# Post-LN stack with two attentions: transposing only the visible 64 by 64 of one probability block

## The reference, cut to what matters

```python
# x: 16 sequences x 256 tokens x 128; 16 heads of 64
h = silu(x @ W1.T + b1) @ W2.T + b2
q, k, v = split(h @ Wg.T + bg)
dots = einsum('bhid,bhjd->bhij', q, k) * 64 ** -0.5
mask = j >= i + 64                      # i: query, j: key
attn = softmax(where(mask, -inf, dots))
out = einsum('bhij,bhjd->bhid', attn, v) @ Wo.T + bo
```

## Time and profile before

| | |
|---|---|
| median of 3 runs | 1578.63 us (1572.71 to 1580.39) |
| the profiled execution's own time | 1580.31 us |
| span of its trace | 1578.5 us |
| busy: PE, PEld, DVE, ACT, POOL | 82%, 61%, 67%, 61%, 50% |
| first attention, about | 39 to 690 us |

### The profile page before, as it was taken

The page is one execution under the profiler, slowest core; times in us unless marked ns, Lnnn a source line. Parts: engine busy times, 40 slices in busy tenths (PEclk is TensorE's granted clock), DMA queues, the critical chain, the costliest instruction groups (busy, mean ns, idle before and its releaser), DMA issues.

```text
span 1578.5 us, 36791 instructions
## 1 busy us (share of the span) xinstructions
PE 1297.7 (82%) x9486; PEld 970.0 (61%) x9486; DVE 1055.8 (67%) x3800; ACT 959.6 (61%) x2716; POOL 796.1 (50%) x913
## 2 busy tenths in 40 slices
PE   7999999999999999836999999604778787787870
PEld 3766666666666666526999999602445455454540
DVE  1677777777777777738766666415777777777646
ACT  5877777777777777614555555302566656566654
POOL 1567777777777777749100000366665655552103
PEclk9999999999999999968999999855899989899985
DMA  9100000000000000021222222122423233232101
GB/s 346 48 8 14 13 13 12 13 12 13 13 13 13 12 12 14 14 81 44 60 66 67 67 67 66 55 52 50 84 50 76 55 69 60 48 76 37 31 1 53
DMA packets 77060, 75.02 MB, mean 48 GB/s; under 512 B 10913, under 2 KB 66977, under 8 KB 75330
## 3 DMA queue, kind: packets, MB, share of 16 engines
q1 hardware_dynamic: 67506, 56.86, 14.1%
q0 software_dynamic: 8192, 16.79, 3.8%
q10 hardware_dynamic: 1296, 0.59, 0.1%
HBM read 46.87 MB, written 27.33 MB: 47 GB/s over the span
## 4 chain that ended last, share of the span: by engine, by line
PE 30%; issue 6%; DVE 6%; ACT 6%; DVEq 3%; POOL 2%; POOLq 1%; SPq 1%; DMA 0%; ACTq 0%
PE psum L818 7%; PE psum L827 6%; PE psum L860 4%; PE psum L849 3%; PE psum L924 3%; ACT qst L1096 2%; POOL yk L568 2%; PE psum L940 2%; PE psum L941 1%; ACT wall L1052 1%; DVE wA L1303 1%; ACT wall L1096 1%; PE psum L882 1%; PE psum L804 1%; DVE xgT L1310 1%
## 5 line engine op out<-in xcount | busy, mean ns | idle before, releaser
L503 POOL TENSOR_SCALAR P<-P,rinv 128x192 f32<-128x192 f32 (+1 forms) x384 | 308.5, 816 | 167.1 <-DVE rinv L1168 165.4
L1008 ACT ACTIVATE P<-shifted,least 128x192 f32<-128x192 f32 (+1 forms) x512 | 240.2, 471 | 128.2 <-DVE least L1154 126.7
L1042 ACT ACTIVATE hid<-psum,wA 128x128 f32<-128x128 f32 x576 | 164.1, 368 | 129.2 <-PE psum L818 129.1
L1352 DVE TENSOR_REDUCE mx<-psum 128x2 f32<-128x512 f32 x256 | 164.5, 686 | 82.1 <-PE psum L924 78.4
L1154 DVE CUSTOM_DVE_ANT_0 shifted<-psum,band 128x192 f32<-128x192 f32 (+1 forms) x512 | 168.8, 385 | 30.6 <-PE psum L696 30.4
L1052 ACT ACTIVATE wall<-psum 128x1024 f32<-128x1024 f32 x128 | 131.0, 1024 | 84.6 <-PE psum L849 82.2
L818 PE MATMUL psum<-xgT,wA 128*128 128x128 f32 x1152 | 158.4, 281 | 13.0 <-DVE xgT L1310 12.3
L493 POOL DMA_INDIRECT xs<-x1c,pos x128 | 127.9, 999 | 56.1 <-issue 28.3
L827 PE MATMUL psum<-wB,hid 128*128 128x128 f32 x1152 | 153.3, 277 | 0.0
L818 PEld LDWEIGHTS psum<-xgT,wA 128*128 128x128 f32 x1152 | 141.6, 193 | 17.4 <-DVE xgT L1310 12.1
L568 POOL DMA_INDIRECT yk<-ys,posc x128 | 124.0, 969 | 49.0 <-issue 33.5
(11 more groups left out here) (246 smaller groups left out, 2678.4 us busy)
## 6 DMA issues: line engine op xcount, KB each, us to landing
xg<-xs SPq DMA_DIRECT2D x144, 64.0 KB, 1.8
ys<-yrow SPq DMA_DIRECT2D x72, 128.0 KB, 1.9
wall<-in_wall SPq DMA_DIRECT2D x1, 8232.0 KB, 36.7
qkd<-parts SPq DMA_DIRECT2D x32, 192.0 KB
qst<-qkd SPq DMA_DIRECT2D x66, 64.0 KB
wall<-qkd SPq DMA_DIRECT2D x35, 64.0 KB
kst<-qkd SPq DMA_DIRECT2D x11, 192.0 KB
hT<-in_xT SPq DMA_DIRECT2D x4, 512.0 KB, 5.6
```

What stands on the lines that cost most here:

```text
L503: g.tensor_scalar(x, x, rinv[:, par, n:n + 1], None, ALU.mult).then_inc(s["pn_ready"], 1)
L1008: last = sc.activation(P[:, par, it, h, 0:w], shifted[:, par, it, h, 0:w], ACT.Exp, scale=-1.0, bias=least[:, par, n:n + 1], accum_out=row ...
L1042: sc.activation(hid[:, p % 4, f, :], UP[two][:, at:at + GT], ACT.Gelu, bias=wA[:, p % 4, F + f:F + f + 1]).then_inc(s["hid_ready"], 1)
L1352: v.tensor_reduce(out=mx[:, :, h], in_=SB[(par + 1 + h) % 3].rearrange("q (i n) -> q i n", i=TT), axis=mybir.AxisListType.X, op=ALU.max).t ...
```

## The change

At head pair steps after the very first, the block of queries 0 to 127 and keys 128 to 255 (`jt` = 1, `it` = 0) is no longer transposed whole. Its quarter with queries 64 to 127 and keys 128 to 191 is transposed alone, with the matching 64 by 64 of the identity. It is written to partitions 0 to 63 and columns 64 to 127 of the bank. The first pair (step 1 of sequence 0) still transposes all of the block, which leaves the zeros in partitions 64 to 127. No wait, no semaphore, no other engine's instruction is changed, and the order of the eight transposes stays: for each head jt = 0 with it = 0 and 1, then jt = 1 with it = 0 (the changed one) and it = 1.

```diff
                             need(pe, ev, pair(b, p, -1))
+                            first = isinstance(b, int) and 8 * b + p == 1
                             for jt in range(TT):
                                 for it in range(TT):
                                     c0 = (N if jt == 0 else 0) + it * 128
-                                    last = nc.tensor.transpose(bk[:, c0:c0 + 128], P[:, par1, it, h, jt * 128:(jt + 1) * 128], ident[:, :])
+                                    if it < jt and not first:
+                                        last = nc.tensor.transpose(bk[0:WINDOW, c0 + WINDOW:c0 + 128], P[WINDOW:128, par1, it, h, 128:N - WINDOW],
+                                                                   ident[WINDOW:128, WINDOW:128])
+                                    else:
+                                        last = nc.tensor.transpose(bk[:, c0:c0 + 128], P[:, par1, it, h, jt * 128:(jt + 1) * 128], ident[:, :])
                             last.then_inc(s["pt_mm"], 1)
```

## The result

The changed kernel takes 1603.93 us (median of 4 runs, 1601.17 to 1604.73), the one before 1575.67 on the same count of runs (1569.31 to 1580.39). The ratio is 1.0179 with an interval of 1.0136 to 1.0221, so between 21 and 35 us slower; forecast were 27.8. The forecast time was 1606.

The account below looks back on a forecast made before the run. PE's stream was taken to bound the attention stage, with a few waits for VectorE. 15 x 1.69 = 25.3 us plus 2.5 for sequence 0 gave 27.8 us more, 1606 us, 1.8% slower; range 1594 to 1630.

Parts of the forecast that it names:

- PE sets the pace: First attention stage: PE busy 38.80 of 40.27 us per sequence, so distances between PE instruction starts decide gain or loss.
- The price, 0.21 us per head: Transposes of each head: PE time added by two new changes of shape, 0.538 us against 0.327 before; 0.42 per pair.
- three terms: Per head, start to start: second transpose to small 0.202, small to fourth 0.175, fourth to next 0.161 us.
- Two passes: Rival: small transpose runs as a plain two-pass float32 matmul, 0.58 us per pair, 40 us in all, 1619; chance 0.12.
- Steps 6 and 7 hidden: Their added 0.84 us goes whole into PE's waits of 1.53 us for VectorE's chain from step 6's scores.
- steps 3 and 4 hidden: Their added 0.84 us fits PE's waits of 1.05 us for VectorE's chain from step 3's scores, 0.2 to spare.
- 1.69 us per sequence: Cost of uncovered steps 5, 0, 1 and 2, 4 x 0.42; over sequences 1 to 15, 25.3 us.
- the open steps: Steps 5, 0, 1 and 2, where VectorE itself waits for PE and nothing was to cover the added time.
- The last sequence as the others: Its PE waits are longer, 1.13 and 1.67 us, but at the same steps 5 and 7, so it was counted alike.
- the terms of the sum: Sequence 0 without cover, 6 x 0.42 = 2.5 us; sequences 1 to 15, 1.69 us each; together 27.8.
- The clock: Rival: drains lower the attention stage's granted clock from 2.4 GHz, up to 0.4 us per sequence for each 1%; chance 0.03.
- the free change of shape: Rival: a small transpose third of four starts like any other, gaining 7.3 us (1571) or 14 us (1565); chance 0.10.

Follow-up runs that it names:

- twice: Changed kernel with each small transpose issued two times in a row; 42.46 us a sequence, ratio to before 1.0219.
- paired: Changed kernel with the small transposes of both heads side by side, two changes of shape per pair instead of four; 40.57 us a sequence, ratio to before 1.0030.
- hidden_steps: Changed kernel with small transposes at steps 3, 4, 6 and 7 only, whole ones elsewhere; 40.27 us a sequence, ratio to before 0.9998.
- open_steps: Changed kernel with small transposes at steps 0, 1, 2 and 5 only, whole ones elsewhere; 41.57 us a sequence, ratio to before 1.0138.
- steps_012: Changed kernel with small transposes at steps 0, 1 and 2 only; 41.13 us a sequence, one run.
- step_5: Changed kernel with small transposes at step 5 only; 40.69 us a sequence, one run.
- small_last: Changed kernel with both heads' small transposes moved to the end of the eight, at every step; 39.72 us a sequence, ratio to before 0.9958.
- delay_step_0: Kernel before with two redundant whole transposes more at step 0, for head 1; 40.33 us a sequence, ratio to before 1.0005.

## Why the prediction was right

- **PE sets the pace, and the distance between starts is the cost.** Right. The durations would have said the opposite.
- **The price, 0.21 us per head.** Right, with each of its three terms within 4 ns. 0.203 + 0.173 + 0.165 = 0.541 us measured (medians) against the 0.538 of the sum and 0.327 before. twice and paired show that it is the change of shape: the small transpose itself costs 0.056, where 0.054 was taken. The Trainium skill's rule of a drain at a change of tiling mode ("TensorEngine Tiling (Array Packing)", section Tiling Modes, Key Properties) held for 128 by 128 to 64 by 64 and back, 0.09 us each, and not between 64 by 64 and 64 by 128.
- **Two passes, as a rival.** Excluded by the 254 instructions. The restriction of the transpose mode under column tiling, which the Trainium skill states ("TensorEngine Tiling (Array Packing)", section Tile-to-Partition Mapping, Restrictions), cost no second pass here.
- **Steps 6 and 7 hidden, steps 3 and 4 hidden.** The first holds as forecast: 0.63 us of the 1.10 is left. The second holds in hidden_steps, with the timing of the kernel before. In the changed kernel VectorE's chain is 0.41 us shorter, so the cover is 0.64 instead of 1.05 and the two steps add 0.86: 0.21 of it comes through.
- **1.69 us per sequence.** Measured 1.52, and this is the term that was off, and not by its price but by its overlap: 4 x 0.428 = 1.71 for the open steps, less the 0.41, plus the 0.21, is 1.51. The same sum gives 41.57 for open_steps (41.57), 41.14 for steps_012 (41.13) and 40.70 for step_5 (40.69). That the length of VectorE's chain is a constant was the assumption that failed, and what moves with it is an engine that I had not put into it.
- **The last sequence as the others.** Wrong in the traces shown: it took 37.95 us instead of 38.94 (row of the kernel before below), and ran at a granted clock of 1.00 where before had 0.96, that is with a stretch at 1.2 GHz. By the traces the change costs 22.4 us up to the last router count (714.19 against 691.76 us), by the medians of the runs 28. The profiled execution of after took 1601.17 us, the least of its four runs, and that of before 1580.31, as much as its highest (1580.39), which is the size of the difference. I can't split the 28 us finer than the interval. In the traces the parts are these: the scores of the last sequence's step 0 come 25.2 us later than before, where the terms of the sum give 2.5 + 14 x 1.69 = 26.2, and the last sequence, counted at 1.69, gave back 1.0. So the parts were up to a tenth too large and the end was counted wrong. That the whole comes within 1 us of the medians' difference is partly luck; the interval of 21 to 35 us would have taken 25 as well.

```profile
625.70:664.64 38.94, 33.47 (x233) 22.75 (x231) 27.86 (x129) 26.37 (x94) 28.12 (x34) 0.96 0.05 15
```

- **The clock and the free change of shape, as rivals.** Neither came: the granted clock was 1.00 in every mid-stage window shown, and every change into or out of whole-array work paid.

## What to carry to other kernels

Before cutting a matmul or a transpose to a smaller tile inside a stream, read the distance between starts where the array's shape changes now, 0.09 us and an open weight load here. In these runs a cut paid only next to work whose rows it shares or leaves free (0.13 us per pair ahead of the scores, nothing ahead of the product with V), so make as few changes as possible, all small tiles together. And when PE is slowed or sped up, look at where the other engines' instructions fall against each other afterwards: here 0.4 us per sequence hung on that, more than the tile saved.

## What the runs showed of the hardware

- From 64 by 64 to 64 by 128 there was no drain, and a transpose in rows 64 to 127 and a float32 matmul in rows 0 to 63 ran side by side, starts 6 ns apart (small_last). The second transpose, ahead of that matmul in program order, started behind it (429.07 against 428.99 us).
- A 64 by 64 float32 transpose lasts 242 ns behind a whole one, and costs 0.056 us behind one of its kind (twice); between whole ones it costs 0.32 us, of which 0.27 is the change out of whole-array work and back, weight loads included (changed kernel).
- Two more whole transposes at step 0 (0.22 us) lengthened a sequence by 0.06 us, the same two at step 5 by 0.23.
- A VectorE row of 128 by 2 elements (line 87) took 0.57, 0.43 or 0.30 us by where GpSimd's scalings fell (before, delay_step_0, open_steps), and 0.18 in twice; the copy after it started 1.95, 1.80, 1.53 and 1.53 us behind the residual.
